# A planned order for TensorE's work in two attention stages, and maxima turned by VectorE

## The reference

```python
x = x + attn_a(layernorm(x)); x = x + ffn(layernorm(x))
x = x + attn_b(layernorm(x)); x = x + ffn(layernorm(x))
# attn_a: c_kv = x @ W_kv_down; k, v, k_rope from c_kv; q, q_rope from x
scores = einsum('bqhd,bkhd->bhqk', q, k) + einsum('bqr,bkr->bqk', q_rope, k_rope)[:, None]
w = softmax(where(causal, -inf, scores / sqrt(40)), axis=-1)
attn = einsum('bhqk,bkhd->bqhd', w, v)        # then @ W_o
# attn_b: the same without the rotary part, scores / sqrt(8), no W_o
```

## Time and profile before

| what | us |
|---|---|
| median of 3 runs (lowest, highest) | 1206.3 (1200.66, 1209.1) |
| the profiled execution | 1209.04 |
| its span, first to last instruction | 1207.3 |
| TensorE busy, of the span | 1039.5 (86%) |
| VectorE / ScalarE / GpSimd busy | 594.8 / 572.0 / 241.9 |
| stage a, TensorE's first and last matmul start | 72.44 and 389.82 |
| stage b, the same | 668.48 and 964.69 |
| granted TensorE clock, mean | 0.932 |

### The profile page before, as it was taken

How to read it: one execution, slowest core, us unless ns; L and a number is a source line. 1 busy time by engine, 2 the same in 40 slices (tenths; PEclk the granted TensorE clock), 3 DMA queues, 4 the chain that set the end, 5 groups by cost and what they waited for, 6 DMA issues and landing times. The chain is left out here.

```text
span 1207.3 us, 17627 instructions
## 1 busy us (share of the span) xinstructions
PE 1039.5 (86%) x6814; PEld 754.2 (62%) x6814; DVE 594.8 (49%) x1324; ACT 572.0 (47%) x1031; POOL 241.9 (20%) x488
## 2 busy tenths in 40 slices
PE   2724899999998799999985499999999859999998
PEld 0312555555654688899983255555555348889998
DVE  5624567777770744511124376766776174451111
ACT  1300456666666454444433046666666645444442
POOL 4010342344222100201007011222222210020000
PEclk9965899999999699999997679999999959999999
DMA  3333322321000400000002521211100040000001
GB/s 79 70 93 116 53 28 53 54 46 32 6 1 2 140 1 1 2 1 1 1 1 46 129 44 28 28 27 21 22 14 2 1 140 1 1 2 1 1 1 35
DMA packets 29916, 39.95 MB, mean 33 GB/s; under 512 B 4130, under 2 KB 22218, under 8 KB 29642
## 3 DMA queue, kind: packets, MB, share of 16 engines
q1 hardware_dynamic: 27610, 37.63, 14.7%
q10 hardware_dynamic: 2224, 1.20, 0.5%
HBM read 28.07 MB, written 10.49 MB: 32 GB/s over the span
## 5 line engine op out<-in xcount | busy, mean ns | idle before, releaser
L993 PEld LDWEIGHTS f_banks<-f_w,f_h 128*128 128x128 f32 x2048 | 241.1, 192 | 5.7
L993 PE MATMUL f_banks<-f_w,f_h 128*128 128x128 f32 x2048 | 243.4, 276 | 0.0
L1051 ACT ACTIVATE f_h<-f_banks,b_t 128x512 f32<-128x512 f32 x256 | 172.2, 688 | 144.2 <-PE f_banks L980 140.7
L980 PE MATMUL f_banks<-f_xr,f_w1r 128*128 128x512 f32 x768 | 199.7, 407 | 0.0
L762 DVE TENSOR_REDUCE a_mlate<-a_banks 128x2 f32<-128x1024 f32 (+3 forms) x120 | 124.8, 1079 | 81.3 <-PE a_banks L633 65.4
L980 PEld LDWEIGHTS f_banks<-f_xr,f_w1r 128*128 128x128 f32 x768 | 140.1, 193 | 25.0
L762 DVE TENSOR_REDUCE b_mlate<-b_banks 128x2 f32<-128x1024 f32 (+3 forms) x120 | 124.8, 1079 | 61.7 <-PE b_banks L633 46.4
L625 PE MATMUL a_banks<-a_k,a_q 120*128 120x512 f32 (+3 forms) x384 | 107.1, 384 | 45.2 <-POOL a_q L554 17.3
L1103 DVE SCALAR_TENSOR_TENSOR x<-f_banks,gate,x 128x128 f32<-128x128 f32 x160 | 45.1, 344 | 200.5 <-PE f_banks L993 200.5
L668 PE MATMUL a_banks<-a_q,a_k 121*128 121x512 f32 (+3 forms) x384 | 117.4, 388 | 11.0 <-DMA a_q<-a_mt 9.9
L668 PE MATMUL b_banks<-b_q,b_k 121*128 121x512 f32 (+3 forms) x384 | 116.3, 385 | 11.9 <-DMA b_q<-b_mt 10.2
(11 more groups left out here) (202 smaller groups left out, 1068.2 us busy)
## 6 DMA issues: line engine op xcount, KB each, us to landing
f_w<-in_w SPq DMA_DIRECT2D x32, 256.0 KB, 5.6
a_k<-scratch_k SPq DMA_DIRECT2D x24, 128.0 KB
a_q<-scratch_q SPq DMA_DIRECT2D x24, 128.0 KB
b_k<-scratch_kb SPq DMA_DIRECT2D x24, 128.0 KB
b_q<-scratch_q SPq DMA_DIRECT2D x24, 128.0 KB
a_k<-scratch_r SPq DMA_DIRECT2D x18, 128.0 KB
a_q<-scratch_r SPq DMA_DIRECT2D x18, 128.0 KB
scratch_kb<-b_k_hl SPq DMA_DIRECT2D x16, 128.0 KB, 2.8
```

The costliest lines, as they stand in the source:

```text
L980: last = pe.matmul(h_ps[:, j, :], w1r[e % 2][wp][:, j * P:(j + 1) * P], xr[xp][:, chunk(c)], start=(i == 0), stop=(i == 2))
L993: last = pe.matmul(y_ps[:, q % 2, i * P:(i + 1) * P], h[q % 2][:, j, i * P:(i + 1) * P], w2[:, e, j, :], start=(j == 0), stop=(j == HB - 1))
L1051: act.activation(h[q % 2][:, j, :], h_ps[:, j, :], ACT.Gelu, bias=m.b1_t[:, e * HB + j:e * HB + j + 1]).then_inc(gelu_done, 1)
```

## The change

The constants of the order are replaced by `planned()`. It walks through the whole stage with a small model of the engines (`Plan`, costs in ns), and at each step takes, among the next piece, unit, set of values and turn of an output, the one that can start first. A unit's set must still fit in `pt`, and pieces may run 15,000 columns ahead. The model has no loads, stores or rotary casts, and counts a row of maxima as there 2400 ns after VectorE is done. The result is `AFTER` (what stands behind each unit) and `COPIES` (behind which unit ScalarE copies the output).

The maxima of a half now lie in a tile of 128 x 32 (16 columns used, 16 zero), and VectorE transposes it in blocks of 32 x 32 at once after the last piece. The 16 rows then lie in four blocks of partitions, 32 elements each; four DMAs take one block each. PE turns the output in place, in bank 7; values of the next half wait until VectorE has read it (o_free). The tile q2 has its token halves outermost, so its loads come as two DMAs where it was one. In the feed-forward stage only names of semaphores change.

```diff
-LEAD = 17000
-TURN_AFTER = 2
-COPY_O, TURN_O = 5, 8
-BURST = [[(-2, -1), (0,), ()], [(-2, -1), (0,), (), (1, 2), (), (3, 4), ()]]
+LEAD = 15000
+class Plan:
+    COLUMN, LOAD, ENTER, LEAVE, SEEN, BACK = 0.44, 115, 155, 112, 260, 150
...
+        if x == len(PIECES[c]) - 1:
+            self.dve += 150 + 200 * c
+            self.m_there[j] = self.dve + 2400
...
+def planned():
...
+    while units or sets or o < len(HALVES):
+        choice = []
+        if ring and issued < scored + LEAD:
+            choice.append((plan.slot_free(), 0, ring[0]))
+        if o < len(plan.copied):
+            choice.append((plan.o_ready(o), 1, ("o", o)))
+        if sets and plan.values_ready(*sets[0][1:]) is not None:
+            full = units and SET0[units[0][1]] + units[0][2] // GH >= len(plan.valued) + NPT
+            choice.append((plan.values_ready(*sets[0][1:]), -1 if full else 2, sets[0]))
+        if units and SET0[units[0][1]] + units[0][2] // GH < len(plan.valued) + NPT:
+            if plan.score_ready(u) is not None:
+                choice.append((plan.score_ready(u), 3, units[0]))
+        key = min(choice, key=lambda c: (max(c[0], plan.pe + 50), c[1]))[2]
...
 def load_group(eng, m, kind, n, loaded):
...
+            if side == "q":
+                for c in range(2):
+                    eng.dma_start(t[n % NBUF][R2 + HD * i:R2 + HD * (i + 1), c, :, :].bitcast(F32),
+                                  src[:, :, c * CH:(c + 1) * CH]).then_inc(loaded[n % NBUF], 16)
...
 def m_rows(eng, j):
-        eng.wait_ge(ring_done, RING[TURN[j]] + 1)
-        for h in range(GH):
-            eng.dma_start(q2[n % NBUF][M0:M0 + 1, h, c * CH:(c + 1) * CH].rearrange("o (q t) -> o q t", t=P).bitcast(F32),
-                          mt[j % 2][TPC * h:TPC * (h + 1), :].bitcast(F32)).then_inc(m_in[j % 2], 16)
+        eng.wait_ge(m_turned, 4 + j + 1)
+        to = q2[n % NBUF][M0:M0 + 1, c, :, :].rearrange("o h (q b r) -> o (h q) b r", q=TPC, b=4)
+        for b in range(4):
+            eng.dma_start(to[:, :, b, :].bitcast(F32), mt[j % 2][32 * b:32 * b + GH * TPC, :]
+                          ).then_inc(m_in[j % 2], 16)
...
-        def turn_m(j):
...
         def turn_o(i):
             pe.wait_ge(o_copied, i + 1)
-            to = slot(("o", i))
             for t in range(TPC):
-                last = pe.transpose(to[:, 0, t * P:(t + 1) * P], ot[:, t * P:(t + 1) * P], m.ident[:, :])
-            last.then_inc(ring_ready, 1)
+                last = pe.transpose(o_ps[:, t * P:(t + 1) * P], ot[:, t * P:(t + 1) * P], m.ident[:, :])
+            last.then_inc(o_turned, 1)
...
 def values(i, s):
-                    pe.wait_ge(o_copied, i)
+                    pe.wait_ge(o_free, 2 * i)
...
+        def turn_m(j):
+            n, c = HALVES[j]
+            if c == 0:
+                dve.wait_ge(ring_done, RING["piece", j, len(PIECES[0]) - 1] + 1)
+            else:
+                dve.wait_ge(m_joined, late[j])
+            if j < 2:
+                dve.wait_ge(m_turned, 4)
+            else:
+                dve.wait_ge(m_in[j % 2], m_in_count(j - 2))
+            dve.transpose(mt[j % 2][:, :], mfull[c][j % 2][:, :].bitcast(F32)).then_inc(m_turned, 1)
```

More of the change, by code:

```diff
@@ new lines, in planned @@
+def planned():
+    ring = [("piece", j, x) for j, (n, c) in enumerate(HALVES) for x in range(len(PIECES[c]))]
+    units = [("score", i, v) for i, (n, c) in enumerate(HALVES) for v in range(NU[i])]
+    sets = [("values", i, s) for i, (n, c) in enumerate(HALVES) for s in range(len(SETS[c]))]
+    plan, after, copies = Plan(), {-1: []}, {}
+    issued = scored = u = o = 0
+    while units or sets or o < len(HALVES):
[11 more added lines that the diff above has]
+        key = min(choice, key=lambda c: (max(c[0], plan.pe + 50), c[1]))[2]
+        if key[0] == "score":
+            plan.score(*key[1:])
+            scored += set_tiles(HALVES[key[1]][1], key[2] // GH)[1]
+            after[u] = []
+            u += 1
+            units.pop(0)
+            continue
+        after[u - 1].append(key)
+        if key[0] == "piece":
+            plan.piece(*key[1:])
+            issued += 2 * CH
+            ring.pop(0)
+        elif key[0] == "o":
+            plan.turn_o(o)
+            o += 1
+        else:
+            plan.values(*key[1:])
+            sets.pop(0)
+            if len(plan.copied) > len(copies):
+                copies[len(copies)] = u - 1
+    return after, copies
@@ L130 @@
+AFTER, COPIES = planned()
+RING = {}
+for keys in AFTER.values():
+    for key in keys:
+        if key[0] == "piece":
+            RING[key] = len(RING)
 KEEP = 3
@@ L689, in values, with beside @@
             last.then_inc(pv_done, 1)
-        def pieces(u):
-            for j, x in BESIDE[u]:
-                if (j, x) == TURN[j]:
-                    turn_m(j)
+        def beside(u):
+            for key in AFTER[u]:
+                if key[0] == "piece":
+                    max_piece(*key[1:])
+                elif key[0] == "values":
+                    values(*key[1:])
                 else:
-                    max_piece(j, x)
+                    turn_o(*key[1:])
         pe.wait_ge(before.split, before.splits)
         pe.wait_ge(before.copied, NCH)
-        pieces(-1)
+        beside(-1)
         for i, (n, c) in enumerate(HALVES):
@@ L703, in tensor @@
                 score_unit(i, v)
[L704 to L715 removed]
+                beside(UNIT0[i] + v)
     def scalar(act):
@@ L740, in scalar @@
                                scale=scale).then_inc(exp_done, 1)
-                if v == COPY_O and i:
-                    copy_o(i - 1)
-        copy_o(NH2 - 1)
+                for done, unit in COPIES.items():
+                    if unit == u:
+                        copy_o(done)
     def vector(dve):
@@ L747, in take_max @@
             n, c = HALVES[j]
-            at = RING[j, x]
+            at = RING["piece", j, x]
             dve.wait_ge(ring_ready, at + 1)
```

252 lines of the change are left out of this document (132 added, 120 removed).

## The result

The change made the kernel slower: 1232.76 us (1227.59 to 1238.5, 4 runs) against 1207.7 us for the kernel before on the same chip (1200.66 to 1216.62, 4 runs), a ratio of 1.0205 with a 95% interval of 1.0117 to 1.0292. The forecast was 1206.5, its range 1192 to 1218. The profiled execution has a span of 1225.9 us where the kernel before had 1207.3.

What follows compares the result with a forecast made beforehand. TensorE's stream in the two attention stages was taken as the bound (busy 1039.5 of 1207.3 us). Terms gave +6 in the first and -5.5 in the second, together +0.5; from the median, 1206.5 us, range 1192 to 1218.

Steps and rivals of the forecast that it cites:

- a +6: First attention stage: steady gain -10, rows of maxima +1.5, opening +8, late masks +6.5, summed to +6 us.
- b -5.5: Second attention stage: steady gain -10, rows of maxima +1.5, opening +3, summed to -5.5 us.
- Fewer ring waits: Steady stretch: values spread between pieces cut TensorE's waits on VectorE's reductions, -2.1 us per group; exponential waits -0.6.
- The -0.6 for exponentials: Steady stretch: a third off TensorE's 1.9 us per group of exponential waits, as ScalarE is fed more evenly.
- More entries into values: Steady stretch: values in 79 bursts instead of 48, 0.35 us per entry and exit, +1.4 us per group.
- The turn leaves TensorE and the ring: Both stages: 16 short transposes fewer each, -0.2 us per group; VectorE's turn and the output's own bank cost nothing.
- Rows of maxima later than planned: First units of halves: rows take 3.6 us, plan says 2.4, lead falls; +1.5 us per stage, bounds 0 to +5.
- Opening of a: First attention stage's start: pieces left behind waits for exponentials and masks, second half opening near 144, +8 us.
- Opening of b: Second attention stage's start: same order with GpSimd free, nine pieces left instead of five, +3 us.
- Late masks: First attention stage, halves 4, 6, 8: values wait some 3 us for GpSimd's masks behind casts, +6.5 us.
- the second: Every half's first unit: row of maxima becomes the last-ending wait if landing over 1 us slower; +20, 1227 us, chance 0.08.

Runs made afterwards that it cites:

- e9: Kernel before, in its own order, with maxima turned by VectorE and q buffers split, output still turned in the ring: 1192.02 us, ratio 0.9838.
- e3: The changed kernel's new parts, output turned in its own bank included, under the order of the kernel before: 1225.37 us, ratio 1.0125.
- e12: e11 with the output turned in a buffer of the ring and the plan told so: 1193.38 us, ratio 0.9859.
- e4: Kernel before with values of late halves' sets 1 to 4 one by one, 16 more entries per stage: 1213.22 us, ratio 1.0013.
- e1: Changed kernel, GpSimd making a half's masks before the next group's casts, group 1's included: 1208.99 us, ratio 0.9982.
- e7: Changed kernel, masks of halves 1, 4, 6, 8 before the casts, group 1's casts left first: 1219.57 us, ratio 1.0063.
- e11: Changed kernel with e7's mask order, 3900 ns per row (8500 the first) and exponentials from 27.7 us in the plan: 1184.38 us, ratio 0.9778.
- e5: Changed kernel with all masks before the next group's casts and 3900 ns per row in the plan: 1193.64 us, ratio 0.9859.
- e2: Changed kernel whose plan counts a row of maxima as there after 3900 ns, not 2400: 1215.14 us, ratio 1.0029.

## Why the prediction was wrong, step by step

The forecast had a +6 and b -5.5; measured were +17.8 and +3.3, so 20.6 us are missing. **Steps 4 and 7** failed and hold nearly all of them. By what mending each gave back, the rows of maxima cost 7.7 and 8.1 us instead of 1.5 each (12.8 missing), the late masks of halves 1, 4, 6 and 8 14.1 instead of 6.5 (7.6 missing). These are single executions, and b alone reads up to 6.8 us apart with one program, so the split is rough. Behind this sum, two other steps had the wrong cause. (The last line of the sum is also off by 0.3: 1209.0 + 0.5 - 2.7 is 1206.8.)

1. *Fewer ring waits.* The size came out right by luck: 14.8 to 5.0 us, 1.7 us a group where 2.1 was taken. The cause, values spread between the pieces, failed. With the old bursts, in which the same 44 pieces lack values before them, the waits are 6.9 us without the turn of maxima in the ring (e9) and 3.8 with the output out of it too (e3), 8.7 and 5.6 with the issue ahead of pieces. The listed order, with 17 or fewer such pieces and no such issue, has 10.3 in place of the first (e12) and 5.0 in place of the second. So what left the ring took the waits away; the order took none, as far as these runs show (the lead of 17,000 or 15,000 changed with it). The -0.6 for exponentials did not come; the idle time that this step left aside as "issue" has to be counted with it (44.0 to 45.3).
2. *More entries into values.* Taken at 0.35 us each from start to start; e4 puts it at 0.26 in the steady stretch and at 0.14 or less over a stage. In those halves e4's units stood 33.9 us instead of 26.2 and its values 14.4 instead of 17.8 (issue and exponentials together): of what the entries cost the units, the values had in part stood for before.
3. *The turn leaves TensorE and the ring.* This step failed: -0.2 us a group, by the 0.03 to 0.3 us of a short transposition. e9 measures -1.4 a group in b. A turn held one of two places of the ring through its own wait, TensorE's part and VectorE's copy, and TensorE's next pieces stood behind it. That the price is the place and not the transposition is what the ring waits (-7.9 of 7.9 us) speak for; no run kept the one without the other, so it isn't shown. VectorE's turn takes 0.21 us (0.25 was taken). The own bank was rightly costed at nothing under cover (e12), and e3 shows the price when it is gone: 15.4 and 17.7 us a stage over 15 halves, 1.0 to 1.2 each instead of 2.
4. *Rows of maxima later than planned.* Failed, and beyond its upper bound of +5. Beyond the opening, units waited 9.0 us for rows in a and 10.3 in b. In the quiet late halves that was 0.62 to 0.66 us each, "some tenths" as said; 3.35 at half 1 of both stages, and 2.38 (half 4 of a) and 1.91 (halves 2 and 10 of b) where the last of the four DMAs landed 3.0 to 3.5 us after its issue, which the step did not have and for which no run shows the cause. The row is there 3.6 us after VectorE's turn, and the plan, which sets a half's first unit for 2.4 us after it, puts TensorE in front of it in every late half of b. I had the 3.6 us from the earlier trace rows, saw the 2.4, and then priced only the difference in lead. Nor was there cover to lose: in seven of the eight late halves of b the kernel before, too, starts the first unit 0.04 to 0.07 us after the last landing event of its row. At halves 4, 6 and 8 its weight load begins 0.21 to 0.23 us behind the one ahead of it, where that is 0.12 in e9, whose rows lie there 3.0 us early. The form of the row is not the cause. By the events that the landings leave, the last of the four DMAs is through 1.61 us after its issue began in quiet halves of before (3.49 us after the copy), and 1.75 us in after (3.59 us after the turn), for the same 2 KB. By the DMA: Bandwidth & Descriptors page of the Trainium skill, Why small descriptors are slow, transfers within SBUF are exempt from the loss below 512 bytes. The trace nearly agrees: with 128-byte runs a DMA took 0.14 us more and the whole row 0.1. Sixteen source partitions in place of four changed with them, and no run separates the two.
5. *Opening of a.* Half 1 opens at 141.70 against 144 forecast, 9.1 us later into the stage against +8. Right; e1 and e7 show 8.1 of it to be the masks behind group 1's casts.
6. *Opening of b.* +3.8 against +3, right in size. e11 shows the reason, a plan in which exponentials and the first row come too early: half 1 of b opens 8.9 us sooner than in e5, and b is 9.9 shorter.
7. *Late masks.* The waits were there, up to 3.0 us each, but four, half 1 among them (2.4, 2.0, 3.0 and 3.0 us at halves 1, 4, 6 and 8). Each half lost more than its wait: halves 4, 6 and 8 took 26.2, 27.1 and 27.1 us, where late halves without such a wait took 22.6. That values that slip push pieces, and with them rows, behind is the likely reason; no run shows it by itself.

Of the rivals the second named the place (the row as the wait that ends last, +20; by e2 it is 16 in two stages) at 0.08, but for landings over 1 us slower, which the traces don't show. I held late rows and late masks for small or for a rival, and not for a sum.

**What remains of the change.** From the kernel before, VectorE's turn alone gives 0.984. The change as written, with the listed order, loses 3.7% against that. With three facts in it, a row's 3.9 us (8.5 for the first), the start of the exponentials, and the later masks before their casts, it comes to 0.978. In b the two are level (281.8 and 282.9); the difference is in a (307.7 and 312.6).

## What to carry to other kernels

A list scheduler puts work exactly at the edge of its latencies, so a latency that is 1.2 us short cost 0.6 us in each quiet late half here, while the order of e9 has the row 3.0 us early. Check each constant of such a plan against a quiet row of the trace, and give the plan every engine, load and start condition that the consumers wait for. A small operation that passes through a shared ring of buffers can cost far more than its own duration, here 0.7 us a half for a transposition of 0.27 us; the time for which it holds a place is the likely price. And try each part of a change alone under the old order: here one part held more than the whole had promised.

## What the runs showed of the hardware

- A DMA of 2 KB within SBUF as 16 runs of 128 bytes had landed 1.75 us after its issue began, as 4 runs of 512 bytes 1.61 us; four in a row are issued 0.55 to 0.63 us apart with the first form, 0.62 with the second. The 4 runs leave five events on the semaphore, the first 1.0 us after the issue and the other four at 1.56 to 1.61; TensorE's waiting unit starts 0.04 us after the last, so the first is not the landing.
- VectorE turned 128 x 32 elements in blocks in 211 to 214 ns, 32 times.
- The idle time that a weight load shows ahead of the first unit behind values is up to 0.84 us, and the profile puts it down to "issue" or to ScalarE depending on what ended last; only the sum of both can be compared between two orders.
